# The blend's last subtraction writes graph by graph into a separate state buffer, and the transposes back read that buffer

## The reference, cut to what matters

```
h = max(layernorm(x), 0)
r = sigmoid(gi_r + gh_r);  z = sigmoid(gi_z + gh_z);  nn = tanh(gi_n + r * gh_n)
x = x + ((1 - z) * nn + z * h)
h = max(layernorm(x), 0)
x = x + adj @ (h @ W) + bias
```

## Time and profile before

| what | value |
|---|---|
| median of three runs | 347.7 us (345.97 to 348.69) |
| the profiled execution | 345.98 us |
| its span in the profile | 344.1 us |
| TensorE (PE) busy | 331.1 us, 96% of the span |
| VectorE (DVE) busy | 263.2 us, 76% |
| ScalarE (ACT) busy | 220.8 us, 64% |
| GpSimd (POOL) busy | 151.7 us, 44% |

### The profile page before, as it was taken

The page is one execution under the profiler, slowest core; times in us unless marked ns, Lnnn a source line. Parts: engine busy times, 40 slices in busy tenths (PEclk is TensorE's granted clock), DMA queues, the critical chain, the costliest instruction groups (busy, mean ns, idle before and its releaser), DMA issues.

```text
span 344.1 us, 6334 instructions
## 1 busy us (share of the span) xinstructions
PE 331.1 (96%) x2212; PEld 297.5 (86%) x2212; DVE 263.2 (76%) x735; ACT 220.8 (64%) x431; POOL 151.7 (44%) x131
## 2 busy tenths in 40 slices
PE   8699979999999999999999999999999999999995
PEld 5489968799989998899989998899989998899884
DVE  5597987898688976898688977898677968674473
ACT  2958745977775785667775785667776655452443
POOL 7053370035932297035922297036920396055014
PEclk9999999999999999999999999999999999999999
DMA  7900100001310031001210031001100000001001
GB/s 233 339 4 0 61 33 0 2 1 53 102 33 1 3 122 63 0 0 59 99 31 0 4 123 61 0 2 61 65 0 2 0 32 30 3 0 63 0 1 64
DMA packets 7952, 15.04 MB, mean 44 GB/s; under 512 B 1008, under 2 KB 1648, under 8 KB 7792
## 3 DMA queue, kind: packets, MB, share of 16 engines
q1 hardware_dynamic: 7776, 14.62, 12.4%
q10 hardware_dynamic: 144, 0.01, 0.0%
HBM read 10.43 MB, written 4.19 MB: 43 GB/s over the span
## 4 chain that ended last, share of the span: by engine, by line
issue 41%; POOL 30%; PE 13%; DVE 9%; ACT 5%; DMA 1%; POOLq 1%; DVEq 0%; ACTq 0%
POOL x_ring L1350 5%; POOL base L1362 3%; POOL rs L1297 3%; POOL ac L940 3%; POOL px L944 2%; POOL px L934 2%; POOL px L937 2%; POOL base L1365 2%; POOL rs L1302 2%; POOL base L1356 2%; DMA vec<-vec_in 1%; PE pNR L305 1%; PE pNR L303 1%; PE pNR L304 1%; ACT conv_hi L658 1%
## 5 line engine op out<-in xcount | busy, mean ns | idle before, releaser
L1302 POOL TENSOR_TENSOR rs<-ve,neg_half 128x4 f32<-128x4 f32 x15 | 15.6, 1039 | 94.7 <-DVE ve L1086 94.7
L1297 POOL TENSOR_TENSOR rs<-ve,neg_half 128x8 f32<-128x8 f32 (+1 forms) x9 | 15.5, 1720 | 73.0 <-DVE ve L964 73.0
L303 PE MATMUL pP<-cx_hi,conv_hi 128*128 128x256 f32 x154 | 45.1, 293 | 0.0
L305 PE MATMUL pP<-cx_hi,conv_lo 128*128 128x256 f32 x154 | 43.5, 282 | 0.0
L304 PE MATMUL pP<-cx_lo,conv_hi 128*128 128x256 f32 x154 | 43.3, 281 | 0.0
L303 PE MATMUL pQ<-cx_hi,conv_hi 128*128 128x256 f32 x126 | 37.2, 295 | 0.0
L305 PE MATMUL pQ<-cx_hi,conv_lo 128*128 128x256 f32 x126 | 35.4, 281 | 0.0
L304 PE MATMUL pQ<-cx_lo,conv_hi 128*128 128x256 f32 x126 | 35.4, 281 | 0.0
L732 ACT ACTIVATE work<-work,nb,rs 128x128 f32<-128x128 f32 x60 | 24.8, 483 | 15.1 <-DVE nb L1090 15.1
L303 PEld LDWEIGHTS pP<-cx_hi,conv_hi 128*128 128x128 f32 x154 | 29.1, 189 | 0.3
L304 PEld LDWEIGHTS pP<-cx_lo,conv_hi 128*128 128x128 f32 x154 | 29.1, 189 | 0.3
(11 more groups left out here) (275 smaller groups left out, 1071.7 us busy)
## 6 DMA issues: line engine op xcount, KB each, us to landing
x_ring<-x_in SPq DMA_DIRECT2D x16, 256.0 KB, 2.8
adj_ring<-adj_in SPq DMA_DIRECT2D x16, 256.0 KB, 3.0
out<-x_ring SPq DMA_DIRECT2D x15, 256.0 KB, 2.0
work<-conv_in SPq DMA_DIRECT2D x1, 1088.0 KB, 8.0
x_ring<-gate_in SPq DMA_DIRECT2D x1, 576.0 KB, 7.6
out<-x_ring SPq DMA_DIRECT2D x2, 128.0 KB, 1.8
early<-early_in SPq DMA_DIRECT2D x1, 129.5 KB, 3.4
late<-late_in SPq DMA_DIRECT2D x1, 128.0 KB, 7.9
```

Source lines behind the costliest of these rows:

```text
L303: pe.matmul(acc, w_hi, m_hi, start=start, stop=False)
L305: return pe.matmul(acc, w_lo, m_hi, start=False, stop=stop)
L1297: pool.tensor_tensor(rs1[:, lane], ve1[:, lane], neg_half[:, lane], ALU.pow).then_inc(rs1_set, 1)
L1302: pool.tensor_tensor(rs2[g % 2][:], ve2[g % 2][:], neg_half[:, 0:GG], ALU.pow).then_inc(rs2_set, 1)
```

## The change

`zh - cand` is no longer written over `zh`. It goes to a new buffer `state`, of which there is one for all groups, and it is written graph by graph: element `4 n + g` of the sources goes to column `128 g + n`. The two sources are read as before, in order. The transposes back then read 128 adjacent columns of `state`. Because there is one `state` only, VectorE waits in front of the subtraction until the transposes of the group before are done (`o_placed` at least g).

```diff
+        state = sb("state", [128, W])
...
-                    last = pe.transpose(graph(bank, j), lane(zh[g % 2], j), ident[:])
+                    last = pe.transpose(graph(bank, j), graph(state[:], j), ident[:])
...
                 have(dve, zn_set, g + 1)
-                dve.tensor_tensor(zh[g % 2], zh[g % 2], cand[g % 2], ALU.subtract).then_inc(oT_set, 1)
+                have(dve, o_placed, g)
+                dve.tensor_tensor(state[:].rearrange("p (g n) -> p n g", g=GG), zh[g % 2].rearrange("p (n g) -> p n g", g=GG),
+                                  cand[g % 2].rearrange("p (n g) -> p n g", g=GG), ALU.subtract).then_inc(oT_set, 1)
```

## The result

The changed kernel takes 349.18 us (median of 18 runs) against 348.21 us of the kernel before, run 18 times beside it. The ratio is 1.0036, with a 95% interval of 1.0019 to 1.0052: slower by 0.7 to 1.8 us, within the 1% case that was forecast, and less than the forecast's 2.7 us. The profiled execution took 349.19 us, its span is 347.4 us.

What follows compares the result with a forecast made beforehand. TensorE is nearly full (96% busy), and VectorE's stream is on the path where TensorE waits for it. 9 x 0.34 - 0.05 - 0.3 = +2.7 us gives a median of 350.4 us, range 346.8 to 353.8 us.

Steps and rivals of the forecast that it cites:

- d: Time added to each of the 16 VectorE subtractions by writing with hops: 0.34 us, bounded by 0 and 0.59 us.
- Weight loads: Transposes back: loads fall to 140 ns, 0.03 to 0.04 us gained for each of nine groups, about -0.3 us.
- Price of the hops: VectorE's subtraction: 0.34 us more, from the weight load's 48% ratio on 692 ns; 0.27 us by the column.
- A nanosecond more on L1068 is a nanosecond more of the whole: Odd group's subtraction, steps 1 to 5: all of d exposed through TensorE's wait at L390, five times.
- Waits at L475: First adjacency product waits for ScalarE's second normalisation, six times and once more in step 7; no second d in steps 1 to 5.
- Step 7: Odd group's subtraction: d exposed once; even group's: exposed less 0.05 us of cover up to the weight load's start.
- Hidden places: Even groups' subtractions in steps 1 to 5 and both groups' in step 6: d hidden, costing nothing.
- The last group: At the end TensorE waits for the subtraction and all that follows is a chain: d exposed once.
- The new wait: VectorE's wait before the subtraction for the previous group's transposes: covered by 6 us in step 2, cost nothing.
- Free writes: Rival: VectorE's hopping writes cost nothing, so the change is -0.3 us, 347.4 us; chance 0.10.
- The full slot: Rival: hops cost a full element slot or more, deciding from d = 0.43 us; 352.7 us at 0.59; chance 0.36.
- The loads in full: Rival: each weight load's 68 ns is elapsed time, TensorE gains 4.4 us; 343.3 us with free writes; chance 0.04.

Runs made afterwards that it cites:

- run 18: Not a run's label: part of "run 18 times beside it", the unchanged kernel before, timed 18 times beside the changed kernel; 348.21 us.
- e1: The kernel before with only the weight loads changed: transposes back read 128 adjacent columns, subtraction as it was; 347.04 us, ratio 0.9993.
- e8: The kernel before with ScalarE's copy of the odd group by graphs, ahead of hT, covering two of four graphs in the steps; 347.73 us, ratio 0.9998.
- e9: The kernel before with only the even groups 2 to 12 written graph by graph and turned back by rows; 347.3 us, ratio 0.9991.

## Why the prediction was right, and where its sizes were off

The sign, the case (within 1%) and the places came out as predicted; the size was 2.7 us where the profile has 1.7 and the runs at equal clock about 1.5 (0.7 to 1.8 by the ratio). That 2.7 came as near as it did is partly luck. The prediction wanted d read from the subtraction's own row, and with the 0.406 us of that row its sum gives 9 x 0.406 - 0.05 - 0.3 = +3.3 us, twice what was measured and just short of the 3.5 us at which it would have changed its case. Its 0.34 us, taken from the ratio of a weight load, happens to be what VectorE's stream pays (0.33 us).

- *Weight loads.* Predicted 140 ns and 0.35 us from transposes to the next product, nine groups, -0.3 us. The changed kernel shows 140 ns and 106.49 - 106.14 = 0.35 us; alone (e1) they are worth 0.37 us in the profile and 0.3 to 0.6 us at equal clock. Right, within that. And 64 x 68 ns = 4.4 us of load time went while 0.4 us of elapsed time came, so it was right to read starts and not durations.
- *Price of the hops.* Predicted d = 0.34 us, measured 0.406 us on the instruction's record. For the record the term was too small; the weight load's ratio was the better guide than its nanoseconds per column (0.27 us), and neither reached it. For the stream 0.34 us was right: the next instruction starts 0.33 us later. The prediction made no difference between the two.
- *"A nanosecond more on L1068 is a nanosecond more of the whole."* This step failed in size. The record grew by 0.41 us, VectorE's stream by 0.33 (the next instruction starts further ahead of the recorded end), and the first 0.12 of that lay behind ScalarE's hT (e8). Five steps at 0.2 instead of 0.34 us are the main part of the difference. My row search stopped at "no idle time in front of L984" and didn't ask whether ScalarE's copy ended at the same moment. The signs that I had named came (the wait at L390 from 0.42 to 0.70 us, the idle time at L984 shorter by 0.4 us), and the wait's growth still overstates the steps', since part of it is TensorE's own gain.
- *Waits at L475.* "Once more, on the matmul's own row, in step 7" counted one wait twice: the sixth of the loads' waits is the one in step 7, and the matmul's row there shows the same wait. Step 6 has none, and TensorE waits for nothing in it, so the gain of its odd group's transposes counts too: -0.08 us measured where -0.03 was predicted.
- *Step 7.* Odd group: VectorE's next instruction starts 0.93 instead of 0.61 us behind the subtraction's start, +0.32, and is exposed, as predicted. Even group: predicted cover 0.05 us, and TensorE's gap grew from 0.24 to 0.41 us, by 0.17 only. The row of the changed kernel shows why:

```profile
330.16 0.42 PEld L469 LDWEIGHTS pH<-ident,state 128*128 128x128 f32 x4 [0.44 <-DVE state L1070]
330.17 0.65 PE L469 MATMUL pH<-ident,state 128*128 128x128 f32 x4
```

  The row before, whose load started at 326.93:

```profile
327.17 0.63 PE L468 MATMUL pH<-ident,work 128*128 128x128 f32 x4
```

  The load was 0.4 us late, but before it ran 327.17 - 326.93 = 0.24 us ahead of its matmul, and that lead is used up first. I had measured the cover to the load's start; it ends at the matmul's.
- *Hidden places.* Steps 1 to 5's and step 6's even groups: confirmed by e9. Step 6's odd group: confirmed by the table (-0.08 us).
- *The last group.* +0.38 us to its transposes, near d.
- *The new wait.* The profile of the changed kernel shows no wait in front of any subtraction (0.5 us of idle time over all 16, as before); cost nothing, as predicted. No run takes the wait away alone.
- *The rivals.* Free writes fell with the 1098 ns. The full slot (from d = 0.43) was close in d and far in the sum, since in steps 1 to 5 only half of d reached the end. The loads in full fell with e1.

## What to carry to other kernels

Moving a stride from one engine's reads to another engine's writes moves its price, and the price depends on the engine: here four weight loads paid 0.04 to 0.06 us of elapsed time for single 4-byte elements, a 512-column VectorE operation 0.33 to 0.41 us. What a longer instruction costs is its successor's later start, less whatever other engine's signal that successor would have waited for at the same moment; the idle notes don't show a cover that ends just when the engine comes free. And where one engine's whole stream is the bound, a wait that is removed by reordering comes back at the next meeting point; the step gets shorter only by what leaves the stretch of that stream, and a moved instruction can bring a new wait into it at a place that was free before. Before two executions are compared, sort them by the granted clock: here one fall of it in the opening was worth as much as the whole change.

## What the runs showed of the hardware

- A VectorE subtraction of 512 fp32 columns takes 692 ns with adjacent elements, 694 ns in runs of two, 1098 ns with single-element hops of 512 bytes on the write, 1096 ns with steps of 16 bytes on both reads.
- Behind a hopping write the next instruction starts 0.94 us after its start, behind hopping reads 1.01 us, for the same recorded 1.1 us. Behind the plain subtraction of 0.69 us it is 0.61 us (e8).
- TensorE's weight load of 128 fp32 columns takes 140 ns from adjacent elements and 209 ns with a step of four, but between the starts of four transposes and the next product that is 0.35 against 0.39 to 0.42 us.
- TensorE's granted clock fell to 0.79 on average over 16 to 24 us, over 48 to 56 us, over both or over neither, in the fourteen executions profiled here. The runs of one program, the kernel before, show all three mean clocks, and lie 1.5 to 1.65 us apart by them (345.97, 347.62 and 349.13 us).
